# Softmax reciprocals of the relative attention: exp(−ln) on ACT in place of RECIPROCAL on DVE, output product one slot later

## What is computed

```
scores = einsum('bhqd,bhkd->bhqk', q, k) / sqrt(8)
attn = softmax(scores + bias[None], axis=-1)
out = einsum('bhqk,bhkd->bhqd', attn, v).transpose(...).reshape(B, L, 128)
y = einsum('blc,dc->bld', out, wo) + bo          # then x = x + y
```

## Time and profile before

| | us |
|---|---|
| median of 3 runs | 2583.72 |
| lowest, highest | 2574.14, 2589.09 |
| the profiled execution, its own time | 2577.03 |
| its span in the trace | 2575.2 |
| busy, share of the span | PE 87%, DVE 71%, ACT 42%, POOL 12% |
| attention stage, first and last bias add of L2266 start at | 1768.7, 1999.5 |
| RECIPROCAL of L2282, 16 times, starts from, to | 1785.4, 2001.7 |

### The profile page before, as it was taken

One profiled execution on the slowest core, in us unless ns is written; L12 is line 12 of the kernel. 1 busy time (PEld: TensorE's weight loads), 2 busy tenths in 40 slices (PEclk: granted clock), 3 DMA queues, 4 the chain that ended last, 5 costly groups with the idle time before them and its releaser, 6 DMA issues.

```text
span 2575.2 us, 59885 instructions
## 1 busy us (share of the span) xinstructions
PE 2242.6 (87%) x24537; PEld 1564.4 (61%) x24537; DVE 1826.1 (71%) x4255; ACT 1076.7 (42%) x2825; POOL 308.3 (12%) x535
## 2 busy tenths in 40 slices
PE   6777788998878888887899999976888799999988
PEld 4555534444455545443688888854665578888855
DVE  4444489999846777776777777725887767777776
ACT  2222146566532212113555555443444345555544
POOL 1111000000002333432000000044331000000000
PEclk6555599999877878876999999978999989999999
DMA  2000000000010000002111110005552111111111
GB/s 53 2 2 2 1 1 1 1 1 1 1 45 4 2 2 3 2 2 78 49 34 38 34 38 34 22 19 113 98 97 46 57 34 38 42 38 35 38 49 30
DMA packets 76052, 76.54 MB, mean 30 GB/s; under 512 B 15769, under 2 KB 57073, under 8 KB 74193
## 3 DMA queue, kind: packets, MB, share of 16 engines
q1 hardware_dynamic: 71872, 70.21, 10.7%
q10 hardware_dynamic: 3904, 2.49, 0.4%
HBM read 60.19 MB, written 11.82 MB: 28 GB/s over the span
## 4 chain that ended last, share of the span: by engine, by line
PE 34%; DVE 11%; ACT 6%; issue 4%; DMA 3%; ACTq 1%; SPq 0%; POOL 0%; DVEq 0%; POOLq 0%
PE B L85 33%; DVE work L1981 2%; DMA work<-work 2%; ACT hr L103 2%; DVE work L107 2%; ACT L103 1%; DVE catt L2282 1%; ACT catt L103 1%; DVE work L1985 1%; ACT work L103 1%; DVE catt L2266 1%; ACT lth L103 1%; DVE work L117 1%; ACTq L2253 1%; ACT ltc L103 1%
## 5 line engine op out<-in xcount | busy, mean ns | idle before, releaser
L85 PE MATMUL B<-gr,wres 128*128 128x512 f32 x1248 | 366.4, 422 | 25.4 <-DVE work L107 13.7
L85 PEld LDWEIGHTS B<-G,lw 128*128 128x128 f32 (+1 forms) x3256 | 260.3, 177 | 70.6 <-DVE G L107 55.4
L103 ACT ACTIVATE work<-B 128x512 f32<-128x512 f32 (+5 forms) x460 | 235.4, 531 | 145.7 <-PE B L85 83.5
L85 PE MATMUL B<-G,lw 128*128 128x32 f32 (+1 forms) x3256 | 266.2, 305 | 29.4 <-DVE G L107 27.5
L85 PEld LDWEIGHTS B<-gr,wres 128*128 128x128 f32 x1248 | 234.3, 193 | 90.1 <-DVE work L107 28.8
L85 PE MATMUL B<-work 128*128 128x128 bf16 (+3 forms) x1408 | 262.5, 314 | 27.4 <-DMA work<-work 14.0
L103 ACT ACTIVATE hr<-work 128x512 fp32r<-128x512 f32 x272 | 175.7, 646 | 136.4 <-DVE work L107 82.8
L85 PEld LDWEIGHTS B<-work 128*128 128x128 bf16 (+2 forms) x1408 | 141.9, 127 | 149.3 <-issue 84.3
L103 ACT ACTIVATE lth<-B 128x96 f32<-128x96 f32 (+1 forms) x512 | 106.3, 228 | 273.0 <-PE B L85 273.0
L1981 DVE TENSOR_TENSOR work<-work 128x512 f32<-128x512 f32 x256 | 177.5, 693 | 51.8 <-ACT work L103 45.8
L1972 DVE TENSOR_TENSOR hr<-work,hr 128x512 fp32r<-128x512 f32 x272 | 188.2, 692 | 35.2 <-ACT hr L103 35.1
(11 more groups left out here) (253 smaller groups left out, 3858.1 us busy)
## 6 DMA issues: line engine op xcount, KB each, us to landing
work<-wdr SPq DMA_DIRECT2D x128, 256.0 KB, 3.1
scr<-catt SPq DMA_DIRECT2D x144, 64.0 KB, 2.0
work<-scr SPq DMA_DIRECT2D x16, 384.0 KB
work<-scr SPq DMA_DIRECT2D x16, 192.0 KB
catt<-in_L_ffn_ew SPq DMA_DIRECT2D x24, 128.0 KB, 2.3
work<-scr SPq DMA_DIRECT2D x16, 128.0 KB
out<-work SPq DMA_DIRECT2D x32, 64.0 KB, 2.2
work<-in_x ACTq DMA_DIRECT2D x2, 512.0 KB, 5.4
```

The lines of the kernel that those rows point to most:

```text
L85: return e.matmul(out, lhsT, rhs, start=start, stop=stop, skip_group_check=True)
L103: return e.activation(out, in_, func, bias=bias, scale=scale)
```

## The change

`A_OUT` goes from 11 to 12. DVE's RECIPROCAL goes. ACT gets an Ln of the sums from PSUM into `arc`, a wait for its own Ln, and an in-place Exp with scale −1, at slot 8u + 10, behind the Exp of that slot. DVE's product with `arc` moves to slot 8u + 11 and waits for ACT's Exp, where it waited for PE; the output matmul moves to slot 8u + 12 and DVE's addition to `X` to slot 8u + 13.

```diff
--- before.py
+++ after.py
@@ -140,7 +140,7 @@
 COND2_LAG = 22
 MAMBA_DT_TURNS = 6
 MAMBA_UNIT_TURNS = ((8, 1, 1, 1), (22, 1, 1, 1))
-A_LEAD, A_PROJ, A_VAL, A_TURN, A_OUT = 15, 28, 4, 5, 11
+A_LEAD, A_PROJ, A_VAL, A_TURN, A_OUT = 15, 28, 4, 5, 12
 MIX_K, MIX_T = (0, 28), (24, 0)
 ROUTE_TURN = 9
 APREP_BEAT = 132
@@ -2211,7 +2211,7 @@
                 mm(e, BV[u % 2][:, 0:256], self.awT[3], self.aO, True, True).then_inc(*inc("at.pe", "wo", u))
 
     def attn_act(self, e):
-        at, inc = self.at, self.inc
+        at, inc, then = self.at, self.inc, self.then
         B2, M0, M1 = self.bank[2:4], self.bank[6], self.bank[7]
         for s, n2, n1, pair in self.attn_slots():
             u = pair(A_PROJ)
@@ -2230,6 +2230,13 @@
                 e.wait_ge(*at("at.dve", "b", n2))
                 p = self.aP[n2 % 4].rearrange("p h q -> p (h q)")
                 act(e, p, p, ACT.Exp).then_inc(*inc("at.act", "e", n2))
+            u = pair(2 - A_OUT)
+            if u is not None:
+                e.wait_ge(*at("at.pe", "pv", 8 * u + 7))
+                if u:
+                    e.wait_ge(*at("at.dve", "o", u - 1))
+                then(e, act(e, self.arc, self.bank[4 + u % 2][:, 256:512], ACT.Ln), "at.act", "ls", u)
+                act(e, self.arc, self.arc, ACT.Exp, scale=-1.0).then_inc(*inc("at.act", "rc", u))
             u = pair(A_VAL)
             if u is not None:
                 e.wait_ge(*at("at.pe", "v", u))
@@ -2278,8 +2285,7 @@
             u = pair(1 - A_OUT)
             if u is not None:
                 B = BV[u % 2]
-                e.wait_ge(*at("at.pe", "pv", 8 * u + 7))
-                then(e, e.reciprocal(self.arc, B[:, 256:512]), "at.dve", "rc", u)
+                e.wait_ge(*at("at.act", "rc", u))
                 if u:
                     e.wait_ge(*at("at.pe", "wo", u - 1))
                 e.tensor_tensor(self.aO, B[:, 0:256], self.arc, ALU.mult).then_inc(*inc("at.dve", "o", u))
```

## The result

The changed kernel takes 2590.11 us in the median of 17 runs (2575.03 to 2595.88), the kernel before 2574.07 in 17 (2568.21 to 2589.73). The ratio, estimated over all these runs, is 1.0045, with a 95% interval of 1.0030 to 1.0061: 8 to 16 us slower, most likely 11.6. The two medians by themselves lie 16.0 us apart. The forecast was 2590, a loss of 10.3 us on a kernel that was taken to need 2580.

A forecast was written before the change was run, and what follows sets the result against it. A loop through Exp 3, the turned maxima's DMA and PE's second pass, with Exp 4 behind the same Exp 3, bounds the period. 9.2 us for 14 pairs, 0.2 and 0.9 made +10.3 on 2580.4: 2590 us, range 2572 to 2606.

The forecast's parts named there:

- Two loads a pair, 3.44 us of block: On ACT between Exp 2 and Exp 3: load, Ln, load, Exp and four gaps take 3.44 us, with 108 loads in all.
- one load for an Ln followed by an Exp: Rival on ACT: one table set serves both, block 0.84 us, time 2552 from 2580 us; chance 0.12.
- the drain of 1.38 us a load: Rival on ACT: each table load adds a drain, block 2.76 us longer, some 39 us more; chance 0.02.
- Exp 3 as the point that counts: ACT's Exp in a pair's slot 3: both ways of the period-setting loop lead through its start, forecast 0.66 us later.
- 14 × 0.66 us: Loop term: in the first 14 pairs the block delays Exp 3 and ACT's later work by 0.66 us each, 9.2 us.
- half of it hidden: Rival: SP's loads set the maxima's landing, loop spans two pairs, 14 × 0.33 + 1.1 = 5.7 us, 2586; chance 0.10.
- The end of the stage, 1.8 us: Last pairs: 14th counted at 0.66 us like the others, 15th some 0.2 us, last bare block 0.9 us.
- The added wait: DVE's product in slot 3 waits for ACT; DVE loses some 2 us of unneeded idle time, 0.13 us to spare, no cost.
- the later slot: Product, output matmuls and addition to X move one slot later; costed at nothing beyond the 0.66 us.

The follow-up runs named there:

- the old slot: Changed kernel with A_OUT 11: ACT's Ln and Exp stay, DVE's product waits for them in the same slot, ahead of bias add 3; 2611.96 us, ratio 1.0137.
- four Copies: Changed kernel with the Ln replaced by a Copy from PSUM and four in-place Copies, logarithm left out, no loads between Exps; 2579.11 us, ratio 1.0021.
- two other kernels with a block of this length: Changed kernel with DVE's reciprocal back for the last three pairs, ratio 1.0008; changed kernel with Ln replaced by seven Copies, six in place, ratio 1.0050.
- slot 6: Changed kernel with A_OUT 16: loads, Ln and Exp in slot 6 in place of slot 2, DVE's product in slot 7; 2595.83 us, ratio 1.0076.
- behind the DMA issues: Changed kernel with A_TURN 6 and ACT's block moved behind the turned maxima's copy and three DMA issues (also called maxima ahead of the block); 2603.2 us, ratio 1.0107.
- six Copies: Changed kernel with the Ln replaced by a Copy from PSUM and six in-place Copies, logarithm left out, no loads between Exps; 2588.43 us, ratio 1.0050.

## Why the prediction was right, point by point

**Two loads a pair, 3.44 us of block: right.** 108 loads (why the compiler placed two, and whether one set could have served both functions, no run shows); Ln 0.385 and Exp 0.418 us where 0.381 and 0.415 were taken from the nearest rows; the block 3.43. The Trainium skill's rule of one load for an Ln followed by an Exp ("ScalarE: Activation LUTs", Table sets: the hidden batching unit) does not hold for this program's loads: 32 more for 16 pairs. Nor does the drain of 1.38 us a load show that the Trainium skill has (the same page, What ACT_TABLE_LOAD costs): Ln follows the load within 0.02 us, and Copies of the same length cost the same.

**Exp 3 as the point that counts: right in the main.** Copy for Ln and the old slot moved the time by what the point moves, −27 us forecast and −1.01% (26 us) measured, and 1.2% forecast (32 us) and 1.37% (35 us) measured, the second with a clock of 0.89 that no forecast had. Taking the maxima out from behind it removed the DMA wait. But it isn't the only point: with four Copies Exp 3 came 0.27 us earlier than before and the periods were 0.3 us longer.

**14 × 0.66 us: too high.** Over the 13 periods it was 0.50 a pair, 6.5 us, and over the first twelve 0.32, which is the 0.33 of the rival *half of it hidden*; two other kernels with a block of this length have 0.48 and 0.49 there. So the loop's term lies between the forecast and that rival. Issue to PE's start was 6.74 to 6.94 us in four of the six pairs that waited for it and 7.22 and 8.07 in the others; the 7.1 to 7.4 of the earlier trace rows were two of eight pairs that had 6.75 to 8.14 (their middle 7.3, after the change 6.85). How much of the 0.66 the landing hid was not measured by itself.

**The end of the stage, 1.8 us: wrong, 7.4.** This is the mis-sized term: "the 15th has no maxima behind it; ACT … catches up but for some 0.2 us", and the 14th counted like the others. The 14th pair is the one whose idle time on ACT was 2.09 and not 2.69 us, which I had seen and counted alike. Behind it PE has no first passes, stands for 3.47 us, and then runs at the lower clock for nearly 7 us. The 13th period already pays 2.7 us and not 0.66. Too much in one term and too little in another made the sum of 10.3 meet 11.6: that is luck. So is the time: I took 2580.4 us for the kernel before, whose median here is 2574.07, and the medians' difference is 16.0 and not 10.3.

**The added wait and the later slot at nothing: right in the first eleven pairs.** DVE waits 34.8 us in 15 waits, and bias add 4 isn't late by them there, with 0.14 us of reserve. In the 12th and 13th pair it comes 0.63 us later than before and in the 14th 1.33, so there the term isn't nothing; how much of the end's 7.4 us is this wait and how much PE's for the turned maxima was not taken apart. In slot 6 and behind the DMA issues the same wait, with the lower clock behind it, went with the loss.

## What to carry to other kernels

Work taken off a busy engine is worth what it delays. Here taking 28 us off DVE won nothing where they became pieces of 3.4 us on ACT ahead of the same Exp, while leaving them on DVE and letting the Exp or the maxima pass ahead of them, by one constant, won 0.6 and 0.9%. Look first for the chain through one period and for what can go ahead of what, and only then for another engine. And size the last rounds of a pipeline by themselves: what covers a wait in the middle is missing there.

## What the runs showed of the hardware that was not expected

PE's granted clock fell behind stops of this size. After 3.47 us of waiting it was 0.50 for nearly 7 us (1996.6 to 2003.4). In the kernel before it fell to 0.50 for some 3 us behind each of the two longest waits for the maxima's DMA from 1785 on (2.12 us up to 1933.28 and 1.99 up to 1964.79), and the period with the first of them took 17.3 us where its neighbours took 14.6 and 15.0. It isn't so each time: with six Copies a wait of 2.01 us had no such stretch behind it. In the kernels in which PE stood some 2 us or more in nearly each pair, the mean over the stage was 0.92, 0.89 and 0.89 (maxima ahead of the block, slot 6, old slot), against 0.98 before and after the change, and groups of four matmuls of 0.39 us took 0.63. There PE not only waited but also worked slower behind the wait. That period, before (granted clock 0.90 in the mean):

```profile
1921.51:1938.85 17.34, 14.17 (x209) 9.65 (x208) 12.64 (x19) 7.00 (x18) 4.85 (x12) 0.90 0.51 97
```
